# A two-layer graph network on one core: layer 0's rows turned through DRAM, head norms summed as rows, inverse roots by ln, exp and a Newton step

## What is computed

```python
h = maximum(layernorm(x), 0)                     # layer 0
q, k, v = h @ Wq, h @ Wk, h @ Wv                 # 4 heads
x = x + softmax(where(adj, q k^T / 8, -max)) v @ Wo + bo
h = maximum(layernorm(x), 0)                     # layer 1
m = h @ map_w.T + map_b                          # 8 heads of 64
n = m / maximum(norm(m, per head), 1e-8)
cos = n n^T;  q = m @ q_w.T + q_b;  k = m @ k_w.T + k_b
p = softmax(where(adj, -1e10, q k^T / 8)) * keep
A = (cos * ~adj > 0.1) * p
x = x + relu((A @ (h @ gcn_map_w.T + b)) @ gcn_W.T / (sum(A) + 1))
```

## Time and profile before

| | |
|---|---|
| median of 3 runs | 3766.14 us (3765.32 to 3766.64) |
| the profiled execution | 3767.53 us, span 3765.7 us |
| busy PE, DVE, ACT, POOL | 3665.0, 2723.6, 1695.4, 1357.2 us |
| granted clock of PE, mean | 0.994 |
| transfers | 381.35 MB, 101 GB/s |

### The profile page before, as it was taken

How to read it: one execution, slowest core, us unless ns; L and a number is a source line. 1 busy time by engine, 2 the same in 40 slices (tenths; PEclk the granted TensorE clock), 3 DMA queues, 4 the chain that set the end, 5 groups by cost and what they waited for, 6 DMA issues and landing times.

```text
span 3765.7 us, 101867 instructions
## 1 busy us (share of the span) xinstructions
PE 3665.0 (97%) x31020; PEld 3224.1 (86%) x31020; DVE 2723.6 (72%) x9432; ACT 1695.4 (45%) x5075; POOL 1357.2 (36%) x2069
## 2 busy tenths in 40 slices
PE   8999999999999999999999999999999999999997
PEld 5888888888888888888888888888888888888885
DVE  3777777777777777777777777777777777777765
ACT  2444444444444444444444444444444444444443
POOL 2333433433433333334334334334333333343331
PEclk9999999999999999999999999999999999999998
DMA  2223323233233233333232332322332333332323
GB/s 94 91 96 106 99 99 107 94 108 102 96 112 102 96 109 100 102 104 104 97 107 98 100 107 94 109 102 96 112 102 96 108 100 102 103 104 98 107 86 107
DMA packets 250601, 381.35 MB, mean 101 GB/s; under 512 B 41328, under 2 KB 173968, under 8 KB 250576
## 3 DMA queue, kind: packets, MB, share of 16 engines
q1 hardware_dynamic: 250304, 380.73, 30.4%
q0 software_dynamic: 272, 0.30, 0.0%
HBM read 179.61 MB, written 167.77 MB: 92 GB/s over the span
## 4 chain that ended last, share of the span: by engine, by line
PE 89%; DVE 5%; issue 4%; DMA 1%; DVEq 1%; POOL 0%; ACT 0%; SPq 0%; POOLq 0%; ACTq 0%
PE bank L949 35%; PE bank L957 19%; PE bank L973 14%; PE bank L981 8%; PE bank L942 7%; PE bank L1090 3%; DVE h L675 1%; DVE x_mid L824 1%; PE bank L1024 1%; PE bank L1102 1%; DVE rel L794 1%; PE bank L898 1%; PE bank L1096 1%; DVE mv L669 0%; DVE rec L785 0%
## 5 line engine op out<-in xcount | busy, mean ns | idle before, releaser
L605 ACT ACTIVATE att<-att,nmax 128x256 f32<-128x256 f32 x1024 | 508.1, 501 | 83.5 <-DVE nmax L760 83.5
L771 DVE SCALAR_TENSOR_TENSOR att<-bank,att 128x256 f32<-128x256 f32 x1024 | 404.9, 421 | 33.0 <-ACT att L605 18.3
L949 PE MATMUL bank<-gT,w_k 128*128 128x256 f32 x3072 | 417.2, 285 | 0.5 <-DVE k L841 0.5
L949 PE MATMUL bank<-gT,w_q 128*128 128x256 f32 x3072 | 414.6, 284 | 2.7 <-DVE w_k L698 1.4
L949 PEld LDWEIGHTS bank<-gT,w_map 128*128 128x128 f32 x3072 | 370.7, 188 | 34.3 <-issue 25.8
L949 PE MATMUL bank<-gT,w_map 128*128 128x256 f32 x3072 | 396.9, 285 | 1.1 <-DVE gT L801 1.1
L949 PE MATMUL bank<-hT,w_qkv 128*128 128x256 f32 x3072 | 392.6, 284 | 4.4 <-DVE hT L801 4.4
L949 PEld LDWEIGHTS bank<-gT,w_k 128*128 128x128 f32 x3072 | 386.7, 189 | 8.2 <-DVE k L841 0.7
L957 PE MATMUL bank<-w_v,gT 128*128 128x512 f32 x1536 | 385.2, 399 | 0.0
L949 PEld LDWEIGHTS bank<-hT,w_qkv 128*128 128x128 f32 x3072 | 373.2, 189 | 13.6 <-DVE w_o L689 4.8
L949 PEld LDWEIGHTS bank<-gT,w_q 128*128 128x128 f32 x3072 | 380.3, 189 | 3.7 <-DVE w_k L698 2.2
(11 more groups left out here) (136 smaller groups left out, 7042.9 us busy)
## 6 DMA issues: line engine op xcount, KB each, us to landing
scratch<-att SPq DMA_DIRECT2D x256, 512.0 KB, 2.6
uT<-scratch SPq DMA_DIRECT2D x1024, 128.0 KB, 3.0
x_in<-x SPq DMA_DIRECT2D x64, 512.0 KB, 3.7
x_res<-x_mid SPq DMA_DIRECT2D x64, 512.0 KB, 2.9
out<-x_res SPq DMA_DIRECT2D x64, 512.0 KB, 2.8
adj<-adj SPq DMA_DIRECT2D x64, 64.0 KB, 1.9
att<-gcn_map SPq DMA_DIRECT2D x1, 1024.0 KB, 10.9
att<-map_rows SPq DMA_DIRECT2D x1, 1024.0 KB, 6.4
```

What stands on the lines that cost most here:

```text
L605: s_.activation(e_sl, e_sl, ACT.Exp, bias=nmax1[:, p, c, e:e + 1], scale=-1.0, accum_out=esum1[:, p, c, e:e + 1]).then_inc(exp1_done, 1)
L771: v_.scalar_tensor_tensor(e_sl, in_blocks(gram_bank[e][:, c * N:c * N + N]), COS_THRESHOLD, e_sl, ALU.is_gt, ALU.mult, accum_out=usum1[:, ...
L949: last = t_.matmul(dst, w(ws, k)[:, t * 128:t * 128 + 128], rhs[:, rs, k, :], start=(k == 0 and i == 0), stop=(k == KT - 1 and i == 2))
```

## The change

Layer 0's h is no longer turned by PE. ACT normalises the rows with the relu in it (`norm0`: scale rstd, bias `shift0` = -mean * rstd, which two new POOL instructions make), DVE transposes the 32x32 blocks (`hflip0`, `hflip1`), SP writes the tile to DRAM (`hsend`) and fetches it back turned (`hfetch`, 4 transfers), and ACT and DVE split it in `hT` (`ht0a`, `ht0b`) in the next round. In the first round alone PE still transposes it.

The head norms: ACT writes, after each `m`, the square of the same PSUM tile as fp32r (`sq_high`); POOL squares as before and subtracts to get `sq_low`. `ss` is 8 matmuls of 256 columns with `head_rows` as 8-wide weights, whose result is 8 rows. The inverse root is ln and exp(-0.5 .) on ACT (`root`) and a Newton step of four instructions on POOL (`pow`). The turn of the factors is gone: DVE splits the rows in `rt` from SBUF. The five tables of steps are new as a whole.

```diff
@@ SP @@
+                    elif kind == "hsend":
+                        sp.wait_ge(h_flipped, C * n + C)
+                        sp.dma_start(scratch_h[:, :, :], h_flips[:, :, :, :, :].rearrange("p b c k f -> p b (c k f)")).then_inc(h_sent, 16)
+                    elif kind == "hfetch":
+                        sp.wait_ge(h_sent, 16 * n + 16)
+                        for cols in range(4):
+                            sp.dma_start(h_turned[32 * cols:32 * cols + 32, :, :, :, :].rearrange("p r c k f -> p r (c k f)"),
+                                         scratch_h[:, cols, :].rearrange("(r p) x -> p r x", p=32)).then_inc(h_in, 16)
@@ POOL @@
+                g.tensor_tensor(shift0[:, :], mv[:, :, 0], rstd[:, :], ALU.mult).then_inc(shift_done, 1)
+                g.tensor_scalar(shift0[:, :], shift0[:, :], -1.0, 0.0, ALU.mult, ALU.add).then_inc(shift_done, 1)
...
-                        g.tensor_tensor(msq[:, t, :], m32[:, t, :], m32[:, t, :], ALU.mult).then_inc(msq_done, 1)
+                        g.tensor_tensor(msq[:, t, :], m32[:, t, :], m32[:, t, :], ALU.mult).then_inc(square_done, 1)
+                        g.tensor_tensor(sq_low[:, t, :], msq[:, t, :], sq_high[:, t, :].bitcast(F32), ALU.subtract).then_inc(msq_done, 1)
...
-                        g.tensor_tensor(rn[:, :], ssq[:, :], minus_half[:, :], ALU.pow).then_inc(rn_done, 1)
+                        pool.wait_ge(root_steps, 2 * n + 2)
+                        g.tensor_tensor(term, rn, rn, ALU.mult).then_inc(rn_steps, 1)
+                        g.tensor_tensor(term, term, ssq, ALU.mult).then_inc(rn_steps, 1)
+                        g.tensor_scalar(term, term, -0.5, 1.5, ALU.mult, ALU.add).then_inc(rn_steps, 1)
+                        g.tensor_tensor(rn, rn, term, ALU.mult).then_inc(rn_steps, 1)
@@ ACT @@
+                    elif kind == "norm0":
+                        act.wait_ge(shift_done, 2 * n + 4)
+                        act.wait_ge(product_full, in_psum(n, "ht1b"))
+                        for c in range(C):
+                            s_.activation(h_flips[:, :, c, :, :], x_in[:, c, :].rearrange("p (k b f) -> p b k f", b=4, f=32), ACT.Relu,
+                                          bias=shift0[:, c:c + 1], scale=rstd[:, c:c + 1]).then_inc(h0_ready, 1)
...
+                        s_.activation(sq_high[:, t, :], bank[bank_of[kind]][:, 0:N], ACT.Square, bias=bias_m[:, t:t + 1]).then_inc(m_ready, 1)
+                    elif kind == "root":
+                        act.wait_ge(product_done, out_of_psum(n, "ss"))
+                        s_.activation(term, ssq, ACT.Ln).then_inc(root_steps, 1)
+                        act.wait_ge(root_steps, 2 * n + 1)
+                        s_.activation(rn, term, ACT.Exp, scale=-0.5).then_inc(root_steps, 1)
@@ DVE @@
+                    elif kind in ("hflip0", "hflip1"):
+                        dve.wait_ge(h0_ready, C * n + C + c + 1)
+                        v_.transpose(blocks, blocks).then_inc(h_flipped, 1)
...
                     elif kind == "rt":
-                        v_.tensor_copy(rnT[0:H1, :], full[0:H1, 0:N]).then_inc(rt_high, 1)
+                        dve.wait_ge(rn_steps, 4 * n + 4)
+                        v_.tensor_copy(rnT[0:H1, :], rn).then_inc(rt_high, 1)
@@ PE @@
                     elif kind == "ss":
-                        for t in range(KT):
-                            for c in range(C):
-                                last = t_.matmul(full[:, c * H1 + 2 * t:c * H1 + 2 * t + 2], msq[:, t, c * 128:c * 128 + 128], half_of[:, :], start=True, stop=True)
-                    elif kind == "rt":
-                        for c in range(C):
-                            last = t_.transpose(full[0:H1, c * 128:c * 128 + 128], rn[:, c * H1:c * H1 + H1], ident[:, :])
+                        for i, part in enumerate((sq_high, sq_low)):
+                            for t in range(KT):
+                                last = t_.matmul(full[0:H1, 0:N], head_rows[:, t, :], part[:, t, :], start=(i == 0 and t == 0), stop=(i == 1 and t == KT - 1))
@@ the table of DVE, the end of a round @@
-        "norm0", "k0", "rt", "bc0", "bc1", "k1", ("back", 3)
+        ("factor", 3), "k0", "q1", "hflip1", "rt", "bc0", ("back", 3), "bc1", "k1"
```

More of the change, by code:

```diff
@@ L51, in gnn_two_layers @@
     TENSOR = [
[5 rows of a table removed]
[4 rows of a table added]
+        ("back", 3)
     ]
     SCALAR = [
[4 rows of a table removed]
[4 rows of a table added]
     ]
     VECTOR = [
[L65 to L70, removed]
-        "norm0", "k0", "rt", "bc0", "bc1", "k1", ("back", 3)
[5 rows of a table added]
+        ("flip_a", 3), ("back", 1), "stats0", ("cos_b", 3), ("flip_b", 3), ("factor", 2), "ss", "q0", ("back", 2), "hflip0",
+        ("factor", 3), "k0", "q1", "hflip1", "rt", "bc0", ("back", 3), "bc1", "k1"
     ]
     POOL = [
-        ("unit", 0), "mask0", ("unit", 1), "sum0", "mid", "sum1", "sum2", "sum3", "rstd1", ("back", 0), "m0", ("back", 1),
-        "m1", "m2", "m3", "rstd0", "pow", ("back", 2), "mask1", ("back", 3)
+        ("unit", 0), "mask0", "mid", ("unit", 1), "sum0", "sum1", "sum2", "sum3", ("back", 0), "rstd1", "m0", "m1", "m2", "m3",
+        "rstd0", ("back", 1), "pow", ("back", 2), "mask1", ("back", 3)
     ]
@@ L83, in gnn_two_layers @@
     OWN = [s for s in PRODUCTS if isinstance(s, str)]
+    LAST_OF_HT = max(("qk0", "qk1", "qk2", "qk3", "v0", "ss"), key=OWN.index)
     LATER = [s for s in PRODUCTS if isinstance(s, tuple)]
@@ L283, in steps @@
             return [s for s in order if (isinstance(s, tuple) and a is not None)
-                    or (isinstance(s, str) and n is not None and (more or s not in ("x", "adj", "stats0", "rstd0", "norm0")))]
+                    or (isinstance(s, str) and n is not None and (more or s not in ("x", "adj", "stats0", "rstd0", "norm0", "hflip0", "hflip1", "hsend", "hfetch")))]
         def in_blocks(ap):
@@ L442, in _ @@
                             pattern=[[-1, 128]], channel_multiplier=1).then_inc(made, 1)
-            g.memset(half_of[0:64, 0:1], 1.0).then_inc(made, 1)
-            pool.wait_ge(made, 6)
-            g.memset(half_of[64:128, 1:2], 1.0).then_inc(made, 1)
+            for e in range(2):
+                if e == 1:
+                    pool.wait_ge(made, 6)
+                for t in range(KT):
+                    last = g.memset(head_rows[64 * e:64 * e + 64, t, 2 * t + e:2 * t + e + 1].bitcast(F32), 1.0)
+                last.then_inc(made, 1)
             pool.wait_ge(made, 7)
@@ L830, in body @@
                         normalise(2 * n + 1, x_mid)
-                    elif kind == "norm0":
-                        normalise(2 * n + 2, x_in)
                     elif kind == "stats0":
@@ L983, in values @@
                 return last
+            pe.wait_ge(h0_ready, C)
+            for c in range(C):
+                for k in range(KT):
+                    last = t_.transpose(bank[2 + c][:, k * 128:k * 128 + 128], h[:, c, k * 128:k * 128 + 128], ident[:, :])
+                last.then_inc(hT_full, 1)
             def body(a, n, more):
@@ L1033, in body @@
                         empty(a, n, kind)
-                        for chunks in (range(2), range(2, 4)):
-                            pe.wait_ge(product_done, out_of_psum(n, "ht0a" if chunks[0] == 0 else "ht0b"))
-                            last = project(full[:, 0:N], lambda s2, k: w_qkv[:, s2, w, k, :], t, hT, chunks)
+                        pe.wait_ge(hT_done, C * n + C)
+                        last = project(full[:, 0:N], lambda s2, k: w_qkv[:, s2, w, k, :], t, hT)
                         last.then_inc(product_full, 1)
                     elif kind == "v0":
-                        pe.wait_ge(product_done, out_of_psum(n, "ht0b"))
+                        pe.wait_ge(hT_done, C * n + C)
                         empty(a, n, kind)
```

113 lines of the change are left out of this document (84 added, 29 removed), and 22 rows, old and new, of tables (SCALAR, TENSOR, VECTOR).

## The result

The changed kernel takes 3906.68 us (median of 4 runs, 3905.68 to 3908.48), the kernel before 3766.24 us in the same comparison: a ratio of 1.037, 95% interval 1.036 to 1.039. It is slower, as predicted, but by 140 us and not by 45.

A forecast was written before the change was run, and what follows sets the result against it. PE, busy 97% of the span, was taken as the bound. Waits of 64 x (1.7 + 0.5 + 0.2) = 154 us, less 112 spared, plus 3, gave 45 us more: 3811 us, 8-in-10 range 3715 to 3900.

The forecast's parts named there:

- PE waits 7.2 - 5.5 = 1.7 us: Before bc0: factors ready 7.2 us after ss ends, PE's other work covers 5.5; 1.7 us a round, bounds 0 and 4.5.
- The length of the chain: From the end of ss over DVE, ACT, POOL and DVE to bc0: 7.2 us, against 5.5 us of PE cover.
- The table loads: ACT's two loads around the logarithm, 1.28 us each: the first nearly hidden, the second bare on the chain.
- The rival without the second load: On ACT between logarithm and exponential: load costs nothing, bc0 waits 0.4 us, 3729 us; chance 25%.
- The rival with a longer stop of ACT: Each table load stops ACT for as much again as its row, both on the chain: 3975 us; chance 12%.
- PE spared: Transposes of layer 0's h, old ss and turn of factors gone, 8 matmuls added: net 1.76 us a round.
- Small waits: PE waits for banks mid-round, 0.5 us, and after layer 1's transposes, 0.2 us, each round.
- the wait before layer 1's transposes: PE's existing wait behind the second layer norm stays the same, 0.84 us.
- h through DRAM: Spill and fetch of layer 0's h take 7.2 us in all and are just hidden, ending last if 0.6 us longer.
- the rival of the late h: Transfers of h 2 us longer make qk0 wait 1.4 us a round: 3899 us; chance 8%.

The follow-up runs named there:

- experiment 1: Changed kernel with the one activation table set holding ln and exp loaded once at the start: 3758.63 us.
- experiment 2: Changed kernel with the 12 matmuls of k1 done twice in each of 63 rounds: 3842.69 us.
- experiment 7: Experiment 4 with the one table set holding ln and exp loaded at the start: 3838.10 us.
- experiment 10: Kernel before the change with POOL's pow done twice in each round, the first result unused: 4011.15 us.
- Experiment 5: Experiment 1 with rt put ahead of hflip1 on DVE: 3821.18 us.
- experiment 6: Changed kernel's tables with the norms of the kernel before, only h through DRAM, and DVE's k1 ahead of bc0: 3770.59 us.
- experiment 9: Experiment 8 with the Newton step as three DVE instructions in rt instead of four on POOL, rt and factor 3 moved: 3702.61 us.
- Experiment 4: Kernel before's tables with only the new head norms (squares on ACT, row sums, root, Newton on POOL) and two table loads: 3996.42 us.
- experiment 8: Experiment 1 with layer 0's statistics and norm0 earlier, both hflips ahead of ss, and ht0a, ht0b first in ACT's round: 3754.56 us.

## Why the prediction was right in direction and short in size

- **The step that failed** is "PE waits 7.2 - 5.5 = 1.7 us", multiplied by 64 and taken as the whole price. The wait was 2.24 us a round (143.5 us, not 109), and behind it the granted clock fell, which the sum had no term for: 79 us. These two are 34 + 79 = 113 us, more than the 96 that were missing, since the small waits came out below their price. Experiments 1, 2, 7 and 10 show the second part. Nothing in the trace of before had a wait over 0.85 us in the middle of the run, so the price was not to be read there; but the page shows the clock in every profile, and a forecast with a repeated 2 us stop of PE should have carried a rival for it.
- **The length of the chain.** From the end of `ss` (1937.51) to `bc0` (1945.06) are 7.55 us, priced at 7.2, and the cover is 5.41, priced at 5.5. Up to POOL's end the sum is right within 0.15 us (1943.38 - 1937.51 = 5.87, priced 6.0). What was short is DVE. `norm0` takes 0.75 us a chunk and not 0.55, but ACT comes to it 0.2 us earlier, and `hflip0` starts at 3.5 as priced. From there to the end of `hflip1` DVE takes 2.86 us (1941.04 to 1943.90) where I had 2.6: `factor` is 0.75 and not 0.6, and the flips are 0.63 and 0.70. So `hflip1` ends at 6.39 and not 6.2; then the cast 0.49, a gap of 0.16 and 0.45 where I had 2 x 0.41 without a gap, and 0.13 to PE. Experiment 5 shows that the order of `rt` and `hflip1` was not the limit by itself; behind it stood the cast against POOL.
- **The table loads** did what their row said: 1.28 us each, the first hidden, the second not. The rival without the second load said 3729 us; experiment 1 took it away and came to 3759, since the wait left was 0.98 us and not 0.4. The rival with a longer stop of ACT gave 3975 us and is refuted by the rows: each activation starts 0.01 to 0.04 us after its load ends.
- **PE spared.** 0.94 us for `ss`, no transposes of h, no turn: as priced, 1.76 us a round.
- **Small waits.** Predicted 0.5 + 0.2 a round, and the wait before layer 1's transposes unchanged. The remainder of the sum is 3905.4 - 3765.7 = 139.7, less 143.5 and 79, plus 112: 29 us or 0.45 a round. By place, from starts: the product behind the transposes, `m0`, is 0.2 late (1987.47 - 1986.35 = 1.12, where a `cos` takes 0.9), `ss` 0.2 where I had nothing; the old wait of 0.84 is now 0.32 before the transposes and the rest before `score 3` and behind `back 1` (1.23 and 0.75 us from start to start, the 0.32 included; a `value` takes 1.01 and a `back` 0.14 at the least in the trace of before). Experiments 6 and 9, with 58 and 50 us of it, show that this alone costs as much as the transposes of h gave.
- **h through DRAM** was hidden, and its price was right: 7.1 us from the issue of the spill to the last landing, where I had 7.2, and 3.1 us of DVE idle where I had 3.4. The slack was not 0.6 us: h had landed 2.3 us (median) before ACT took it in the changed kernel, and 0.9 us in experiment 1. That the rival of the late h gave 3899 us, near the measured time, is chance: in the rounds behind the first, PE has one wait of 0.9 us for it.

Open: which of the small waits of the new order could be removed. No run took them apart. Open too: why a fifth of the long waits left the clock alone.

## What to carry to other kernels

A wait of the matrix engine that comes back every round has two prices: its length, and, once it is long, the work behind it at half clock. Here 2.2 us of wait cost 3.5 us on the mean of all rounds, and 1 us cost 1. When pricing a chain across engines, sum it against its cover, look at what stands ahead on each engine that it passes, and at what the neighbour on the next engine does in that moment. Look into the list of instructions for table loads, and name the set where functions alternate.

## What was not expected of the hardware

- The granted clock of PE fell from 1.00 to 0.50 around the end of a wait of 1.9 to 2.5 us, mostly after PE had started again: in 48 of 64 waits of the changed kernel and 56 of 64 of experiment 10 the stretch at half clock begins between 0.3 us before and 1.8 us after the new start. Experiment 4, with waits of 1.9 to 2.0 us, has them at 50 of 64. Waits of 0.6 to 1.1 us in the middle of the run left it alone, every one (kernel before, experiments 1, 2, 7 and 8); between 1.1 and 1.9 us nothing was measured. Redundant matmuls in the wait made the kernel 64 us faster.
- A DVE cast of 8x256 from SBUF took 0.28 us by itself, and beside a POOL addition of 128x256 it ended 0.25 us after that addition did, whatever its start: 0.49, 0.90 and 0.90 us in the three pairs of rows above (1944.32 against 1944.07; 1964.74 against 1964.49; 1930.42 against 1930.17), and 0.24 to 0.26 us in all 441 pairs of the seven kernels that have them. It does not run slower, it waits. The Trainium skill ("SBUF — State Buffer", Who interferes with whom) says that a DVE cast and GpSimd can want the same port pair, and that the later one blocks until the first is done; the rows agree.
- ACT took 0.80 us for a chunk of 512 columns with scattered output and two per-partition operands, where one of `unit`'s takes 0.625. No run here separates the two.
